# Middle stage of an adaLN block: high one-hot rows of three chunks on GpSimd, more low ones on DVE, ACT's first ones behind its last copy

## What is computed

```python
    h = _layernorm(x, axis=-1) * (1 + ca) + sa
    x = x + ga * _L0_attn_ref(h, L0_attn_w_qkv, L0_attn_w_out, L0_attn_b_out)
    h = _layernorm(x, axis=-1) * (1 + cb) + sb
    x = x + gb * _L0_ffn_ref(h, L0_ffn_Wg, L0_ffn_bg, L0_ffn_W1, L0_ffn_b1, L0_ffn_W2, L0_ffn_b2)
...
        gate_probs = jax.nn.softmax(x @ Wg + bg, axis=-1)
        _, top_idx = jax.lax.top_k(gate_probs, k)
...
        h = jax.nn.gelu(jnp.einsum('bsf,efh->bseh', x, W1) + b1)
        expert_out = jnp.einsum('bseh,ehf->bsef', h, W2) + b2[None, None]
        return jnp.einsum('bsef,bse->bsf', expert_out, selected)
```

## Time and profile before

| | |
|---|---|
| median of 3 executions | 815.82 us |
| lowest, highest | 813.88, 817.16 us |
| the profiled execution | 815.38 us |
| its span | 813.6 us |
| PE busy | 755.6 us (93%) |
| DVE busy | 607.7 us (75%) |
| ACT busy | 463.9 us (57%) |
| POOL busy | 339.7 us (42%) |

### The profile page before, as it was taken

How to read it: one execution, slowest core, us unless ns; L and a number is a source line. 1 busy time by engine, 2 the same in 40 slices (tenths; PEclk the granted TensorE clock), 3 DMA queues, 4 the chain that set the end, 5 groups by cost and what they waited for, 6 DMA issues and landing times.

```text
span 813.6 us, 16799 instructions
## 1 busy us (share of the span) xinstructions
PE 755.6 (93%) x5848; PEld 689.2 (85%) x5848; DVE 607.7 (75%) x1321; ACT 463.9 (57%) x841; POOL 339.7 (42%) x291
## 2 busy tenths in 40 slices
PE   5889999999999889985699999999999999999992
PEld 4667778788888678973599999999999999999992
DVE  6899999988899724699677767676676876776652
ACT  4465565756645431349556666575565765765461
POOL 2341314323321101500256564646555565656553
PEclk9999999999999989986799999999999999999997
DMA  7500000000000133591253532626335244333332
GB/s 279 169 1 1 1 1 2 1 2 1 1 2 1 52 105 124 175 250 17 93 140 66 145 62 43 168 40 168 57 89 121 47 116 93 46 47 60 60 48 40
DMA packets 45650, 59.71 MB, mean 73 GB/s; under 512 B 8018, under 2 KB 38804, under 8 KB 45460
## 3 DMA queue, kind: packets, MB, share of 16 engines
q0 software_dynamic: 14400, 21.98, 15.0%
q1 hardware_dynamic: 31188, 36.93, 14.3%
HBM read 40.63 MB, written 18.27 MB: 72 GB/s over the span
## 4 chain that ended last, share of the span: by engine, by line
PE 73%; DVE 18%; issue 5%; POOL 1%; DMA 1%; ACT 1%; SPq 0%; DVEq 0%; POOLq 0%; ACTq 0%
PE ps L1670 24%; PE ps L1684 23%; PE ps L1484 7%; PE ps L1442 6%; PE ps L1505 3%; PE ps L1644 2%; DVE q_max L939 2%; PE ps L1567 2%; PE ps L1493 2%; DVE at_hi L1223 2%; DVE q_sum L946 2%; DVE k_blk L1049 2%; DVE q_exp L940 1%; DVE ln_s L903 1%; PE ps L1556 1%
## 5 line engine op out<-in xcount | busy, mean ns | idle before, releaser
L852 ACT ACTIVATE hid<-ps,b_col 128x256 f32<-128x256 f32 (+1 forms) x232 | 106.1, 509 | 112.7 <-PE ps L1670 108.3
L1684 PE MATMUL ps<-w_hi,hid_hi 128*128 128x256 f32 x544 | 153.5, 282 | 0.0
L1684 PE MATMUL ps<-w_hi,hid_lo 128*128 128x256 f32 x544 | 151.2, 278 | 0.0
L1684 PE MATMUL ps<-w_lo,hid_hi 128*128 128x256 f32 x544 | 151.2, 278 | 0.0
L1363 DVE TENSOR_TENSOR hid_lo<-hid,hid_hi 128x512 fp32r<-128x512 f32 (+1 forms) x116 | 91.0, 784 | 74.7 <-ACT hid_hi L856 74.3
L1670 PE MATMUL ps<-xT_hi,w_hi 128*128 128x256 f32 (+1 forms) x464 | 140.4, 302 | 1.6 <-DVE xT_lo L1317 1.6
L1670 PE MATMUL ps<-xT_hi,w_lo 128*128 128x256 f32 (+1 forms) x464 | 140.1, 302 | 0.0
L1670 PE MATMUL ps<-xT_lo,w_hi 128*128 128x256 f32 (+1 forms) x464 | 140.1, 302 | 0.0
L538 POOL TENSOR_TENSOR q_n<-q_exp,q_rec 128x1024 f32<-128x1024 f32 x32 | 61.0, 1905 | 174.7 <-DVE q_rec L947 174.7
L613 POOL DMA_INDIRECT out<-y,y_id x68 | 117.1, 1722 | 40.1 <-POOL y_id L608 17.6
L601 POOL DMA_INDIRECT listed<-xrows,gid x87 | 95.8, 1101 | 42.3 <-POOL gid L597 24.6
(11 more groups left out here) (215 smaller groups left out, 1462.4 us busy)
## 6 DMA issues: line engine op xcount, KB each, us to landing
w_raw<-in_L_ffn_W SPq DMA_DIRECT2D x16, 1024.0 KB
x_all<-in_L_attn_x SPq DMA_DIRECT2D x8, 512.0 KB, 9.4
out<-x_all SPq DMA_DIRECT2D x8, 512.0 KB, 3.0
xrows<-x_all SPq DMA_DIRECT2D x8, 512.0 KB, 4.6
listed<-xrows,gid POOLq DMA_INDIRECT x87
out<-y,y_id POOLq DMA_INDIRECT x68
wqk_raw<-in_L_attn_w_qkv SPq DMA_DIRECT2D x2, 512.0 KB, 6.3
wqk_raw<-in_L_attn_w_qkv SPq DMA_DIRECT2D x1, 1024.0 KB, 10.5
```

What stands on the lines that cost most here:

```text
L852: ins = act.activation(hid[:, m, 0:T], src, ACT.Gelu_apprx_tanh, bias=b1_col[:, e, m:m + 1])
L1684: last = pe.matmul(ps[:, bank, 0:D], a, w_, start=m == 0 and st, stop=m == M - 1 and sp_)
```

## The change

GpSimd gets a `hi_hot` of its own and makes the 24 high one-hot rows of chunks 1, 2 and 3, right after `place(0)`. It signals with a new semaphore, `s_hiP`. DVE keeps the high rows of chunks 0, 4, 5, 6 and 7. Of the low rows DVE now makes chunk 6, k = 1, and both halves of chunk 7; ACT makes chunks 0 to 5 and chunk 6, k = 0. ACT's `lo_hot(0)` moves from behind `copy_T(14)` to behind `copy_T(15)`. PE's order stays, its waits follow the makers.

```diff
@@ -306,6 +306,7 @@
         s_lohi = sem("s_lohi")
         s_abs = sem("s_abs")
         s_hiD = sem("s_hiD")
+        s_hiP = sem("s_hiP")
         s_loA = sem("s_loA")
         s_loD = sem("s_loD")
         s_idx = sem("s_idx")
@@ -572,6 +573,19 @@
             for i in range(BI):
                 pool.dma_start(out[N + i * P:N + (i + 1) * P, :], pad[:, i, 0:D]).then_inc(s_added, 16)

+            def hi_hot(c):
+
+                for k in range(2):
+                    for i in range(CH):
+                        last = pool.tensor_scalar(at_hi[:, c, k, i, :], iota_hi[:, :], spot_hi[:, 0, k, c * CH + i:c * CH + i + 1],
+                                                  token_of[:, c * CH + i:c * CH + i + 1], ALU.is_equal, ALU.mult)
+                    last.then_inc(s_hiP, 1)
+
+            pool.wait_ge(s_iota, IOTAS)
+            pool.wait_ge(s_lohi, 1)
+            for c in range(1, GCH):
+                hi_hot(c)
+
             for c in range(CHUNKS):
                 pool.wait_ge(s_xo[c], 16)
             pool.wait_ge(s_xr, 16 * (BI + CHUNKS + GROUPS))
@@ -801,15 +815,14 @@
                     w_part(0, q - 2)
                 if q == 9:
                     soft(0)
-                if q == 14:
-                    lo_hot(0)
+            lo_hot(0)
             lo_hot(1)
             soft(1)
             lo_hot(2)
             lo_hot(3)
-            for c in range(GCH, CHUNKS - 1):
+            for c in range(GCH, CHUNKS - 2):
                 lo_hot(c)
-            lo_hot(CHUNKS - 1, range(1))
+            lo_hot(CHUNKS - 2, range(1))


             act.wait_ge(s_const, CONSTS)
@@ -1252,21 +1265,20 @@
                     place(0)
                 if q == 14:
                     hi_hot(0)
-                if q == 15:
-                    hi_hot(1)
             spread(1)
             root(1)
             scale(1)
             first(1)
             second(1)
             weigh(1)
-            hi_hot(2, (0,))
             place(1)
-            hi_hot(2, (1,))
-            for c in range(GCH - 1, CHUNKS - 1):
+            for c in range(GCH, CHUNKS - 1):
                 hi_hot(c)
+            lo_hot(CHUNKS - 2, 1)
             lo_hot(CHUNKS - 1, 1)
-            hi_hot(CHUNKS - 1, (1, 0))
+            hi_hot(CHUNKS - 1, (1,))
+            lo_hot(CHUNKS - 1, 0)
+            hi_hot(CHUNKS - 1, (0,))
             link(dve.tensor_tensor(counts_f[:, :], list_next[:, :], list_start[:, :], ALU.subtract))
             link(dve.tensor_tensor(place_of[:, :, :], place_of[:, :, :], bc(counts_f[:, :], 2, [P, E, COLS]), ALU.is_ge))
             link(dve.tensor_tensor(pad_t[:, :], place_of[:, :, :].rearrange("p e c -> p (e c)"), pad_row[:, 0:E * COLS], ALU.mult))
@@ -1603,11 +1615,16 @@
                 cc = c % GCH
                 final = c == CHUNKS - 1
                 for n, k in enumerate((1, 0) if final else (0, 1)):
-                    if final and k == 1:
+                    if final:
+                        pe.wait_ge(s_loD, n + 2)
+                    elif c == CHUNKS - 2 and k == 1:
                         pe.wait_ge(s_loD, 1)
                     else:
                         pe.wait_ge(s_loA, c + 1)
-                    pe.wait_ge(s_hiD, c * 2 + n + 1)
+                    if 1 <= c < GCH:
+                        pe.wait_ge(s_hiP, (c - 1) * 2 + n + 1)
+                    else:
+                        pe.wait_ge(s_hiD, (c - (GCH - 1 if c else 0)) * 2 + n + 1)
                     for i in range(CH):
                         last = pe.matmul(ps[:, IX, 0:E * COLS], at_lo[:, cc, k, i, :], at_hi[:, cc, k, i, :],
                                          start=c == 0 and n == 0 and i == 0, stop=final and n == 1 and i == CH - 1)
```

## The result

The changed kernel takes **819.15 us** (median; 818.87 to 821.54), the kernel before in the same comparison 816.77. The ratio is 1.0041, with a 95% interval of 1.0029 to 1.0054: slower by 3.4 us, 2.4 to 4.4. (The medians alone differ by 2.4 us; the means of the eight executions of each, 819.76 and 816.42, give the ratio.) That lies inside the range, and within the 0.5% to which the prediction gave most of the chance, though two of its steps, GpSimd's price and what a collision costs, were wrong. In the profiled executions the middle stage lost 2.46 us where 1.4 were forecast, and it lost them on another path.

The account below looks back on a forecast made before the run. DVE's chain to the row numbers `ids` bounds the kernel, PE 0.25 us behind. PE's last products put `ids` at 389.3 instead of 387.85: +1.4 us, 817.2 us on the median of 815.82; range 814.2 to 822.8.

Parts of the forecast that it names:

- The last copy, ACT, place(1): Middle stage: copy(15) starts 0.41 us earlier, ACT ends 1.3 us earlier, place(1) comes 0.25 us later.
- 3.1 us taken off DVE before place(1) buy nothing: Twelve high rows leave DVE, but on PE ranks(1) stands behind index(1), which waits for lo_hot(1) to 369.9.
- The clock at the end: PE's last 16 products run at the low clock: 1.45 us lost; about 0.8 if it rises during them.
- rival B: PE's clock is high at the end and collisions stay hidden: -0.2 us, 815.6 us; chance 0.16.
- GpSimd's price: One high row on GpSimd taken as 0.5 us, so 24 take 12 us from 354.7, on no path.
- rival D: GpSimd over 1.1 us a row, its 24 ending after 381, holding PE and DVE's last chunk: +10 and more; chance 0.05.
- The port: At SBUF, GpSimd and DVE instructions wait for each other and alternate: 16.4 collisions of 0.31, 5.1 us on DVE, hidden.
- by that rule hi_hot(0) waits: By the skill page's contention rule, DVE's hi_hot(0) waits for GpSimd; without that, collisions cost under 4 us, hidden either way.
- The sum: `ids` at 389.3 instead of 387.85: +1.4 us, 817.2 us on the median.
- C at 0.76: Rival where collisions decide, over 4 us slower, chance 0.20; at 0.76 us a GpSimd instruction +7.1, 822.9 us.

Follow-up runs that it names:

- two_chunks: The changed kernel, but GpSimd makes the high rows of chunks 1 and 2 only and DVE those of chunk 3; 816.46 us, ratio 0.9999.
- ranks_first: two_chunks with ranks(1) ahead of index(0) on PE; 815.89 us, one run.
- cheap_rows: The changed kernel with GpSimd's 24 rows as multiply and add with zeros, `ids` a ramp, the true lists left out; 816.78 us, one run.
- warm_end: two_chunks with 24 products of 256 columns that nobody reads added on PE behind chunks 2 to 5; 816.59 us, ratio 0.9998.
- prices: The kernel before, with GpSimd making eight forms of instruction, three of each, into buffers that nobody reads; 821.62 us, one run.
- port_only: The kernel before, with GpSimd also making the change's 24 high rows into a buffer that nobody reads; 818.68 us, ratio 1.0020.
- after_warm: The changed kernel with unread products added on PE, around chunks 2 and 3, during the gather and among the expert stage's first transposes; 817.37 us, ratio 1.0006.
- port_long: port_only with four rows to an instruction, 6 of 1024 columns instead of 24 of 256; 821.08 us, one run.

## Why the prediction was right, and where it wasn't

**The last copy, ACT, place(1).** Right. In two_chunks the three came at the recorded hundredths, closer than the clock lets two executions agree, so the last digit is luck. In the changed kernel's own profile the last copy is 0.84 us earlier than that, because PE's clock fell a pair later: the logits of pair 14 took 1.06 us there and 1.88 in two_chunks and before. "3.1 us taken off DVE before place(1) buy nothing" stands, but the order on PE is only 0.5 us of the reason: that is what place(1) waited in the changed kernel (0.49), and what ranks_first won. The collisions, which the prediction counted apart, took most of the rest.

**The clock at the end.** Right as a mechanism, half right for the changed kernel. There it was 0.5 until 387.4 and then 1.0 under the last 16 products, the ones recorded at 0.5; GpSimd's lateness had put 36 in a row, and the clock rose in the middle of them. Where the products set the end (two_chunks) they ran at 0.5 and cost the recorded 1.4; where the clock rose during them (cheap_rows) the recorded 0.8; where it was high (warm_end) -0.2, rival B's value.

**GpSimd's price.** Wrong: 0.5 was taken, 0.35 and 0.76 were the bounds, 1.23 was measured. The bounds came from rows without a comparison, and a comparison more than doubles the instruction. The condition of rival D (over 1.1 us, "the 24 end after 381", "chunk 3's products hold PE and DVE's last chunk") came true word by word, with a chance of 0.05.

**What D costs.** Also wrong, and this saved the forecast. D was given +10 and more; in the profile it cost 1.0 us beyond the forecast, in the timed runs the whole loss of 3.4 (two_chunks is at 0.9999). GpSimd ended at 384.0, 3 us late, and nearly everything behind it was already made: DVE had only 3.4 us of rows and 1.3 of sums left to do. Such a lateness delays what waits for it, not the whole chain.

**The port.** Right at the price that it assumed (5.1 us recorded and, in cheap_rows, measured), wrong in its law. It multiplied by the length of GpSimd's instruction; that holds for the forms it was read from, two-input instructions and copies (prices: 3.16 us of DVE for 3.12 of GpSimd), and for multiply-and-add rows (cheap_rows). Beside is_equal rows a hold was up to 0.32 us, once 0.46, of 1.23, and there were fewer of them. By its law the true price would have meant some 22 us of collisions; port_only had 2.57. The two errors, in price and in law, had opposite signs, and that they offset each other is luck. The section of the Trainium skill that was weighed ("GPSIMD Engine Reference", Key points) names as contending DVE instructions in a two-port mode or with two SBUF inputs. hi_hot's rows, with one tensor input, waited too (4.22 us instead of 2.11 in cheap_rows); whether they run in a two-port mode no run shows, so "by that rule hi_hot(0) waits" came out as said but isn't shown to be for that reason.

**The sum.** +1.4 recorded, +2.46 in the profile, +3.4 (2.4 to 4.4) in the timed runs. That the forecast has the right sign and size is partly luck: its path, ACT and then 16 products at half clock, isn't the one that ended last. The two profiled executions differ by 3.71 us, and that splits up. The stage before gives back 0.45 (spot_lo(0) at 354.03 instead of 354.48). To `ids` 2.46 are lost, of them 1.0 by GpSimd's lateness. From `ids` to the expert stage's first matmul another 0.79 (10.10 instead of 9.31): the third gathered block can be used 7.32 us behind `ids` instead of 6.53. after_warm has 10.05, cheap_rows 9.79, all the others 9.2 to 9.4. So it goes with GpSimd making all three chunks for use (port_only, whose 24 rows nobody reads, has 9.32); why a gather should land later then, no run shows. 0.91 lie behind the first matmul. 0.65 of that would be the expert stage's half-clock stretch, 4.5 us in this profile against 3.2; but that stretch varied from 2.9 to 5.6 us between kernels whose expert stage is the same, so it isn't shown to belong to the change. The range's ends are off by 0.1 to 0.2 us against its own terms (815.6 less half of 3.3 is 814.0, and C at 0.76 was 822.9), which changes nothing.

## What to carry to other kernels

Price an operation on an engine by a row with the same ALU operation, not by the nearest shape; if there is none, time it on that engine before moving work there. A hold read from one kind of instruction can't be carried to another: time that too. Work taken off the engine that bounds a stage is worth only what the next two limits allow: here the others stood 0.25 us behind. In every kernel here in which TensorE waited for the gather, the matmuls behind it ran at half clock for the first 2.9 to 5.6 us; products that nobody reads, put into the wait, took that away.

## What the runs showed of the hardware

- GpSimd's tensor_scalar on 128x256 (prices): 1.22 us with is_equal and multiply, 0.92 with is_equal alone, 0.56 with multiply and add; 128 columns of the first 0.80. A copy took 0.40.
- How long GpSimd holds a DVE instruction on SBUF hangs on GpSimd's operation. Multiply-and-add rows of 0.54 us held, one after another, every DVE row on SBUF alone but the statistics, by about 0.31 (cheap_rows). Three two-input tensor_tensors and three copies held DVE for all their 3.12 us (prices). is_equal rows of 1.23 us held about one small row in four, by up to 0.32 and once 0.46 (the changed kernel), 2.57 us for 24 (port_only); six of 1024 columns held DVE by 0.26 to 0.88 at a time, 3.70 in all (port_long). DVE's statistics rows were not stretched. Which part of the GpSimd instruction does it, no run shows.
- In after_warm PE's granted clock, kept at 1.0 until then by added products, fell to 0.5 at about 384.3, at the end of the 2.17 us in which PE waited for GpSimd, and stood there until 387.7, under the dense products. Kept up to a wait, it didn't last over it.
